# One power instruction of eight columns in place of three in each turn of the dense node path

## The reference, cut to what matters

```
x = layernorm(x + gat(x))            # two attention convolutions
x = layernorm(x + attention(x))
x = layernorm(x + gnn(x))            # its own norm has eps, gamma and beta:
                                     #   out = (out - mu) * rsqrt(var + eps) * gamma + beta
x = layernorm(x + diffuse(x))        # silu(x @ w_in + b_in), six steps
                                     #   term = inv_deg * segment_sum(term[src]) / i
                                     # then out @ w_out + b_out
def layernorm(x):
    return (x - mean(x)) / sqrt(var(x) + 1e-5)
```

## Time and profile before

| | |
|---|---|
| median of 3 runs | 3975.6 us |
| range of the runs | 3973.98 to 3982.41 us |
| profiled execution, its time as a run | 3978.42 us |
| its span | 3976.6 us |
| mean granted TensorE clock | 0.919 |
| busy: PE | 3270.6 us (82%) |
| DVE | 2815.4 us (71%) |
| POOL | 2282.9 us (57%) |
| ACT | 1892.1 us (48%) |

### The profile page before, as it was taken

One profiled execution on the slowest core, in us unless ns is written; L12 is line 12 of the kernel. 1 busy time (PEld: TensorE's weight loads), 2 busy tenths in 40 slices (PEclk: granted clock), 3 DMA queues, 4 the chain that ended last, 5 costly groups with the idle time before them and its releaser, 6 DMA issues. The chain is left out here.

```text
span 3976.6 us, 57087 instructions
## 1 busy us (share of the span) xinstructions
PE 3270.6 (82%) x14868; PEld 2599.0 (65%) x14868; DVE 2815.4 (71%) x7915; ACT 1892.1 (48%) x5401; POOL 2282.9 (57%) x2529
## 2 busy tenths in 40 slices
PE   5999926687675998469999972999999999999775
PEld 4888725575464665237777761878878787878654
DVE  5767668697784666875666651888888888888633
ACT  3777615576232111233333330566656665666455
POOL 4766500587475664133333321878788787878577
PEclk8999959899898999559999995999999999999898
DMA  4887739443574332463333329767767676767654
GB/s 144 245 247 242 225 113 367 128 131 109 153 218 128 93 88 60 140 200 96 114 113 113 111 87 323 228 200 234 227 205 235 201 233 199 233 198 233 188 189 156
DMA packets 690470, 710.73 MB, mean 179 GB/s; under 512 B 73444, under 2 KB 644190, under 8 KB 689796
## 3 DMA queue, kind: packets, MB, share of 16 engines
q1 hardware_dynamic: 592204, 484.13, 39.3%
q0 software_dynamic: 68288, 181.26, 16.1%
q10 hardware_dynamic: 29660, 41.70, 3.1%
HBM read 427.77 MB, written 296.22 MB: 182 GB/s over the span
## 5 line engine op out<-in xcount | busy, mean ns | idle before, releaser
L595 POOL DMA_INDIRECT s_i_messages<-h,table_row x600 | 645.6, 1076 | 192.2 <-issue 81.5
L2610 PE MATMUL s_i_bank<-s_i_messages,s_i_equal 128*128 128x256 f32 x1200 | 363.5, 386 | 78.0 <-DMA s_i_messages<-h,table_row 74.1
L776 PE MATMUL s_n_bank<-w,n_xt 128*128 128x256 f32 x1280 | 308.1, 384 | 21.4 <-DMA n_xt<-in_x_t 21.4
L2647 DVE SCALAR_TENSOR_TENSOR s_i_y<-s_i_bank,s_i_scale,s_i_acc 128x256 f32<-128x256 f32 x600 | 284.5, 475 | 44.1 <-PE s_i_bank L2610 24.5
L794 PE MATMUL s_n_bank<-w_out,n_ht 128*128 128x256 f32 x1280 | 309.9, 386 | 0.9 <-ACT n_ht L804 0.9
L785 PE MATMUL s_n_bank<-n_x3t,w_in 128*128 128x256 f32 x1280 | 304.1, 381 | 0.0
L816 ACT ACTIVATE n_w<-n_w,n_small 128x256 f32<-128x256 f32 x320 | 145.1, 500 | 308.1 <-POOL n_small L843 307.4
L2610 PEld LDWEIGHTS s_i_bank<-s_i_messages,s_i_equal 128*128 128x128 f32 x1200 | 218.6, 193 | 108.5 <-issue 79.5
L776 PEld LDWEIGHTS s_n_bank<-w,n_xt 128*128 128x128 f32 x1280 | 247.2, 193 | 56.7 <-DMA n_xt<-in_x_t 21.8
L794 PEld LDWEIGHTS s_n_bank<-w_out,n_ht 128*128 128x128 f32 x1280 | 247.6, 194 | 36.0 <-ACT n_ht L804 1.3
L785 PEld LDWEIGHTS s_n_bank<-n_x3t,w_in 128*128 128x128 f32 x1280 | 244.3, 191 | 33.9 <-ACT n_x3t L674 0.2
(11 more groups left out here) (426 smaller groups left out, 9401.6 us busy)
## 6 DMA issues: line engine op xcount, KB each, us to landing
h<-s_i_y SPq DMA_DIRECT2D x600, 128.0 KB, 3.2
n_xt<-in_x_t SPq DMA_DIRECT2D x160, 256.0 KB
out<-n_w SPq DMA_DIRECT2D x160, 256.0 KB, 2.2
s_i_equal<-eq_tab SPq DMA_DIRECT2D x600, 64.0 KB
x<-s_x_rows SPq DMA_DIRECT2D x100, 256.0 KB
out<-s_a_hs SPq DMA_DIRECT2D x100, 128.0 KB
proj_dst<-s_a_hd SPq DMA_DIRECT2D x100, 128.0 KB
h<-s_h_rows SPq DMA_DIRECT2D x50, 256.0 KB, 4.0
```

The costliest lines, as they stand in the source:

```text
L595: return net.nc.gpsimd.indirect_dma_start(out, None, table, bass.IndirectOffsetOnAxis(index, 0))
L776: mm = self.nc.tensor.matmul(self.pr[:, g * self.D:(g + 1) * self.D], self.XT[u][:, c, g * P:(g + 1) * P], self.net.w12[:, c, :], start=c ...
L2610: nc.tensor.matmul(banks[r % 4][:, 0:D], EQ[q % NM][:], M[q % NM][:], start=True, stop=True).then_inc(summed, 1)
L2647: V.scalar_tensor_tensor(Y[q % NY][:], banks[r % 4][:, 0:D], scale[:, s, t:t + 1], acc[:, t, :], ALU.mult, ALU.add).then_inc(added, 1)
```

## The change

All three powers of a turn go into one instruction. A tile `powers` of 16 columns is added, one per parity of the turn (not of the unit): columns 0 to 7 take what is to be raised, columns 8 to 15 the result. The two affine forms of unit 0's variance go to columns 0 to 3, the variance of unit -2 to 4 and 5, that of unit -5 to 6 and 7; `powers_of(j, u, lag)` finds the tile of the turn in which a unit stands `lag` turns behind. On POOL `powers` holds for the variance of unit 0, then for that of unit -2, then for that of unit -5, and then issues one power over all columns that the turn has: eight in most turns, six before the sixth turn, four or two in the last ones. One semaphore `powered` counts turns and takes the place of `scaled`, `dev3` and `dev5`. The scales (in the next turn), the third norm and the last norm wait for the turn's count. The two DVE instructions of unit 0's variance, and the others of the variances, are the same in number; they write to the new tile. Order and number of all other steps, the gaps and the DMAs stay.

```diff
--- before.py
+++ after.py
@@ -728,6 +728,12 @@
 class Dense(Unmet):
+    THIRD, LAST = 2, 5
     @classmethod
     def all_units(cls, net):
         return -(-net.N // (cls.G * P))
@@ -740,10 +746,12 @@
         self.XT = self.sb("xt", [P, C, G * P], 2)
         self.W = self.sb("w", [P, G, D], 2)
         self.HT = self.sb("ht", [P, C, G * P])
+        self.V = self.sb("powers", [P, 16], 2)
+        self.powered = self.sem("powered")
         self.xt_in = [self.sem(f"xt_loaded{u}") for u in range(2)]
         self.stored = [self.sem(f"stored{u}") for u in range(2)]
-        self.ht_ready, self.out_made, self.w_made, self.w_ready, self.var5_ready, self.var5_eps, self.dev5, self.o_ready = (
-            self.sem(n) for n in ("ht_ready", "out_made", "w_made", "w_ready", "var5_ready", "var5_eps", "dev5", "o_ready"))
+        self.ht_ready, self.out_made, self.w_made, self.w_ready, self.var5_ready, self.var5_eps, self.o_ready = (
+            self.sem(n) for n in ("ht_ready", "out_made", "w_made", "w_ready", "var5_ready", "var5_eps", "o_ready"))
         self.x3_free = self.w_made
     def banks(self, pr, tp, hd, op):
@@ -751,6 +759,11 @@
     def first_row(self, j, u):
         return min((self.first + 2 * j + u) * self.rows, self.N - self.rows)
+    def powers_of(self, j, u, lag):
+        i = 2 * j + u + lag
+        return self.V[i % 2], i
@@ -810,10 +823,19 @@
             sq = self.nc.scalar.activation(self.squares[1][:, g, :], self.W[u][:, g, :], ACT.Square, scale=self.D ** -0.5, accum_out=self.S[u][:, 36 + g:37 + g])
         sq.then_inc(self.var5_ready, 1)
+    def scales(self, act, j, u):
+        v, i = self.powers_of(j, u, 0)
+        act.wait_ge(self.powered, i + 1)
+        for g in range(self.G):
+            sc = self.nc.scalar.activation(self.Z[u][:, g, :], self.net.bc["gamma"][:], ACT.Identity, bias=v[:, 8 + g:9 + g],
+                                           scale=v[:, 10 + g:11 + g])
+        sc.then_inc(self.t_ready, 1)
     def last_norm(self, act, j, u):
-        act.wait_ge(self.dev5, j * 2 + (u + 1))
+        v, i = self.powers_of(j, u, self.LAST)
+        act.wait_ge(self.powered, i + 1)
         for g in range(self.G):
-            nm = self.nc.scalar.activation(self.W[u][:, g, :], self.W[u][:, g, :], ACT.Copy, scale=self.S[u][:, 40 + g:41 + g])
+            nm = self.nc.scalar.activation(self.W[u][:, g, :], self.W[u][:, g, :], ACT.Copy, scale=v[:, 14 + g:15 + g])
         nm.then_inc(self.o_ready, 1)
@@ -831,16 +853,54 @@
         dve.wait_ge(self.w_made, j * 2 + (u + 1))
         V.tensor_tensor(self.W[u][:], self.W[u][:], self.net.bc["b_out"][:].unsqueeze(1).broadcast_to([P, self.G, self.D]), ALU.add).then_inc(self.w_ready, 1)
+    def var_1(self, dve, j, u):
+        V, s = self.nc.vector, self.S[u]
+        v, i = self.powers_of(j, u, 0)
+        dve.wait_ge(self.var1_ready, j * 2 + (u + 1))
+        V.tensor_scalar(v[:, 0:2], s[:, 0:2], 1 + EPS, EPS * EPS, ALU.mult, ALU.add)
+        V.tensor_scalar(v[:, 2:4], s[:, 0:2], 1 + EPS * (1 + EPS), EPS ** 3, ALU.mult, ALU.add).then_inc(self.scales_in, 1)
+    def var_3(self, dve, ch, j, u):
+        V, s = self.nc.vector, self.S[u]
+        v, i = self.powers_of(j, u, self.THIRD)
+        hold(self.net, dve, ch.sem, ch.base + ch.k)
+        for g in range(self.G):
+            ch(V.bn_aggr(s[:, 24 + 2 * g:26 + 2 * g], s[:, 12 + 6 * g:18 + 6 * g]))
+        ch.wait()
+        V.tensor_scalar(v[:, 4:6], s[:, 25:28:2], EPS, None, ALU.add).then_inc(self.var3_ready, 1)
+        ch.close()
+    def third_norm(self, dve, j, u):
+        s = self.S[u]
+        v, i = self.powers_of(j, u, self.THIRD)
+        dve.wait_ge(self.powered, i + 1)
+        self.past(dve, self.x3_free, j * 2 + (u - 1))
+        for g in range(self.G):
+            nm = self.nc.vector.tensor_scalar(self.X3[u][:, g, :], self.Z[u][:, g, :], s[:, 24 + 2 * g:25 + 2 * g], v[:, 12 + g:13 + g],
+                                              ALU.subtract, ALU.mult)
+        nm.then_inc(self.x3_ready, 1)
     def var_5(self, dve, j, u):
+        v, i = self.powers_of(j, u, self.LAST)
         dve.wait_ge(self.var5_ready, j * 2 + (u + 1))
-        self.nc.vector.tensor_scalar(self.S[u][:, 38:40], self.S[u][:, 36:38], EPS, None, ALU.add).then_inc(self.var5_eps, 1)
-    def pow_5(self, gp, j, u):
-        s = self.S[u]
-        hold(self.net, gp, self.var5_eps, j * 2 + (u + 1))
-        self.nc.gpsimd.tensor_tensor(s[:, 40:42], s[:, 38:40], self.net.neg_half[:, 0:2], ALU.pow).then_inc(self.dev5, 1)
+        self.nc.vector.tensor_scalar(v[:, 6:8], self.S[u][:, 36:38], EPS, None, ALU.add).then_inc(self.var5_eps, 1)
+    def powers(self, gp, j, u):
+        v = self.V[u]
+        bases = []
+        if n := self.at(j, u, 0):
+            hold(self.net, gp, self.scales_in, n[0] * 2 + (n[1] + 1))
+            bases += [0, 4]
+        if n := self.at(j, u, self.THIRD):
+            hold(self.net, gp, self.var3_ready, n[0] * 2 + (n[1] + 1))
+            bases += [4, 6]
+        if n := self.at(j, u, self.LAST):
+            hold(self.net, gp, self.var5_eps, n[0] * 2 + (n[1] + 1))
+            bases += [6, 8]
+        b0, b1 = bases[0], bases[-1]
+        self.nc.gpsimd.tensor_tensor(v[:, 8 + b0:8 + b1], v[:, b0:b1], self.net.neg_half[:, 0:b1 - b0], ALU.pow).then_inc(self.powered, 1)
@@ -895,7 +955,7 @@
             self.var_5(dve, *v)
         gap()
         if third:
-            self.var_3(dve, ch, third[1])
+            self.var_3(dve, ch, *third)
         if v := self.at(j, u, 0):
             self.var_1(dve, *v)
         gap()
@@ -908,12 +968,7 @@
     def turn_gp(self, gp, j, u, gap):
         gap()
         gap()
-        if v := self.at(j, u, 5):
-            self.pow_5(gp, *v)
-        if v := self.at(j, u, 2):
-            self.pow_3(gp, *v)
-        if v := self.at(j, u, 0):
-            self.pow_1(gp, *v)
+        self.powers(gp, j, u)
         gap()
         gap()
```

## The result

The changed kernel takes **4005.7 us** (median of 5 runs, 4004.46 to 4016.24) against 3975.6 (5 runs, 3973.24 to 3982.41): a ratio of 1.0083, 95% interval 1.0070 to 1.0095. It is slower by 30 us, where 3988 was forecast with a range of 3955 to 4020. The profiled execution took 4004.46 us with a span of 4002.6, 26.0 over the 3976.6 of before.

What follows compares the result with a forecast made beforehand. POOL was taken to bound the steady n turn (7.85 us), but not m. Steady n -29, other n turns +17 and m +25 gave +13 us: 3989.6 for the span, 3988 for the median, range 3955 to 4020.

Steps and rivals of the forecast that it cites:

- the wait for unit 0: Third and last norm now need the power that also needs unit 0's variance; variance to third norm 2.13 us.
- POOL's relief: Two fewer POOL issues per turn: 1.64 us for eight columns against 2.41, giving 0.77 us back.
- The new cycle: Chain third norm, unit 0's variance, power, third norm sets the turn: 7.61 us in n, 7.41 in m.
- The power: POOL's single power of eight columns takes 1.64 us, from a line through 2, 4 and 6 columns.
- The holds: Three POOL holds in a row, the late one first: 0.19 us plus 0.13 for each other, 0.45 in all.
- m: Stage beside the gather of out1: turns go from 6.61 to 7.41 us, +25 us in all.
- n steady: Usual turns of the stage beside the diffusion: 120 turns go from 7.85 to 7.61 us, -29 us.
- n, other turns: Short turns at step changes, first turns and long waits in the n stage: +17 us, bounds +5 and +28.
- The step that failed: In SP's queue the store of out waits 0.7 us longer; stores and mask loads behind have tiles of lead.
- Rival A: Further holds are hidden, variance to third norm 1.87 us; PE's 7.41 us decides in n: 3952 us, chance 0.25.
- Rival B: Interface held through the power, so DVE's bias add waits for its end; third norm at 8.30: 4112 us, chance 0.05.
- Rival C: Wait costs more: holds of 0.30 us, a slower power, or PE behind the later silu: 4050 us, chance 0.17.

Runs made afterwards that it cites:

- e2: The changed kernel with the store of out moved to the end of SP's turn: 3973.4 us, ratio 1.0002.
- e3: The changed kernel with two four-column powers, units -2 and -5 first, unit 0 behind; store of out left in place: 3935.4 us, ratio 0.9888.
- e1: The changed kernel with ten buffers instead of five for the diffusion's result tiles: 3971.2 us, ratio 0.9991.
- e4: The changed kernel with store of out last in SP's turn and POOL's holds in the order unit -5, -2, 0: 3943.7 us.
- e7: The changed kernel with two four-column powers, units -2 and -5 first, unit 0 behind, and store of out last: 3933.4 us.
- e5: The kernel before, its store of out held until unit 0's power of the same turn is issued: 3981.3 us, ratio 1.0018.
- e11: The changed kernel with a one-column scratch power added behind the power, in n only: 3999.4 us, ratio 1.0067.

## Why the prediction was right, and what was wrong in it

The range held, and the mechanism that the prediction described is there. That the sign came out is luck all the same. The terms that the forecast was summed from, the wait for unit 0 against POOL's relief, come to nothing together: the changed kernel without the store waits takes 3973.4 us, a ratio of 1.0002 (e2; n -21.5 and m +18.9 in the profiles), where +13 was forecast. The measured +30 is a term that the prediction had put at nothing.

- **The new cycle: right.** All turns of m and n are third norm, variance, holds, power, third norm; POOL stands idle ahead of the power for L861; the silu is covered (L807 waits 2.1 us in all).
- **The power: right.** 1.66 against 1.64 from the line through three sizes.
- **The holds: a size off.** 0.10 each, not 0.13; variance to third norm is 2.08, not 2.13. The plain difference of the earlier trace rows was the measured price; the allowance on top was not in any row.
- **m: +19.4 against +25.** The mean turn is 7.18, not 7.41 (the first 33 intervals): 0.07 by the holds and the power (2.06 from variance to third norm, not 2.13); the rest is third norm to variance, 5.13 and not 5.28. It is 5.21 on average in the kernel before, so the 0.07 for the delayed copy did not come and the stretch got shorter instead; why wasn't separated.
- **n steady: 7.52 against 7.61.** The 0.04 for the gather beside the norm did not come in most turns. That alone would be 120 x -0.33 = -40.
- **n, other turns: +16.8 against +17.** A hit by luck in part: the store waits are in it, and without them it is +14.3 (e2).
- **The step that failed: "In SP's queue the store of out waits 0.7 us longer; the stores and mask loads behind it have tiles of lead."** The 0.7 was right (0.26 to 0.93 behind the third norm). The lead was not counted out: with five buffers it is 4.15 us, not tiles. It lost 0.5 to 0.6, and the landing grew from 2.0 to 3.7 us; with the store as late and the gathers where they were it is 2.2 (e3). Price 32 to 35 us (e2, e1), where the prediction had nothing: n would be 21.5 us shorter (e2) and is 10.8 longer.
- **Rival A** (holds hidden) did not happen, but e4 made it: it needed the late hold to be the last. Its PE floor of 7.41 was too high: 7.86 less 0.45 takes off PE's idle time ahead of the transposes alone, but the transposes themselves are stretched there too (0.49 to the next matmul, 0.44 in e4), and e4's full turn is 7.33. (DVE's 7.25 doesn't follow from its rows either: 7.86 less the 0.65 that it stands is 7.21. Nothing hangs on it.)
- **Rival B** (interface kept to the end) is out: the bias add at 3022.29 ran inside the power at its usual 0.69, as it did in 129 turns of n and 34 of m, and the undisturbed turn is 7.52, not 8.30. The Trainium skill (SBUF — State Buffer, "Who interferes with whom") would have it wait; the trace does not agree where the power is first. What the rows do show is a POOL instruction that starts inside such a DVE add getting longer: the gathers of 1.51 and 1.48 (e7), the power of 1.51.
- **Rival C** (4050): no hold was of that price; the time above the forecast has another source than the one it named.

By parts, against the forecast of +13 for the span: n steady -11, m -6, store waits +34, the tail and the rest -4: +26.

## What to carry to other kernels

Fusing small instructions of several pipeline lags also fuses their due times: the early ones wait for the latest input, here 0.57 us a turn in m, where the 0.77 us of POOL time saved was worth nothing. Fuse only lags whose inputs are ready together, or put the one that is late last in the order of waits. When a wait is added to a step, follow every queue in which that step stands to the last buffer that depends on it, and count lead and landing in us. A late store alone cost little here (5 to 9 us of n in e3 and e5, hardly more than a single profile can be off), and 32 once the gathers started beside it as well. And when an engine waits, compare the wait with the idle time that the engine has behind it in the turn: only what is over it counts.

## What was not expected of the hardware

- POOL's holds (a wait with an increment behind it), one after the other, cost 0.10 us each when they follow a late one in the open (0.39 to 0.19 with two of them moved ahead), and nothing that shows while POOL is busy (L725 starts 0.02 before L843 ends, with a hold between them).
- A power's duration is close to a line over its columns, 0.54 (e11), 0.70, 1.04 (e7), 1.32 and 1.66 us for 1, 2, 4, 6 and 8 of them.
- With the 128 KB tile store issued 1.88 us after the third norm in all three, its landing is 2.2, 3.1 and 3.7 us as the first gather starts 1.14 (e3), 0.67 (e11) and 0.15 us (changed) after it. The gathers' start is not all of it: e5, with its gathers at 1.13 and the store at 1.96, has 2.9.
- An instruction added to POOL each turn did not make the changed kernel slower (3999.4 against 4005.7; the intervals of the two ratios overlap, so that it is faster isn't shown), and two reorderings without any instruction less took off 62.
